# A recurrent cell on one core: VectorE's copy of the state into the operand sets becomes two

## The reference, cut to what matters

```
m = concat([x_t, h]) @ weight + bias         # 256 -> 256
c = tanh(m[128:]); g = sigmoid(m[:128] + 1)
h = g * h + (1 - g) * c                      # the output at t
```

## Time and profile before

| | us |
|---|---|
| median of 3 runs (lowest, highest) | 466.81 (466.53, 467.8) |
| the profiled execution | 467.08 |
| its span, first to last instruction | 465.3 |
| busy: PE, PEld | 347.9, 215.8 |
| busy: DVE | 345.3 (74%) |
| busy: ACT | 274.0 (59%) |
| busy: POOL | 79.4 (17%) |

### The profile page before, as it was taken

One profiled execution on the slowest core, in us unless ns is written; L12 is line 12 of the kernel. 1 busy time (PEld: TensorE's weight loads), 2 busy tenths in 40 slices (PEclk: granted clock), 3 DMA queues, 4 the chain that ended last, 5 costly groups with the idle time before them and its releaser, 6 DMA issues.

```text
span 465.3 us, 11585 instructions
## 1 busy us (share of the span) xinstructions
PE 347.9 (75%) x3776; PEld 215.8 (46%) x3776; DVE 345.3 (74%) x1940; ACT 274.0 (59%) x1020; POOL 79.4 (17%) x152
## 2 busy tenths in 40 slices
PE   1877799787846786846788988988688879777832
PEld 1644465455534453624544645535444446446510
DVE  6577666787899887899888788752851378799883
ACT  2344544436547536546656566736588888953952
POOL 6000000012000012000011100014020034266580
PEclk9999999999999999999999999995769999997966
DMA  7200920001000000000000000000000000000002
GB/s 178 61 2 25 212 40 2 1 8 41 2 0 3 0 2 1 2 1 2 0 2 2 2 1 2 2 1 3 3 2 3 1 2 4 2 0 1 23 1 68
DMA packets 9118, 8.28 MB, mean 18 GB/s; under 512 B 1282, under 2 KB 7700, under 8 KB 9060
## 3 DMA queue, kind: packets, MB, share of 16 engines
q1 hardware_dynamic: 8964, 7.29, 7.0%
q0 software_dynamic: 96, 0.26, 0.2%
HBM read 6.47 MB, written 1.08 MB: 16 GB/s over the span
## 4 chain that ended last, share of the span: by engine, by line
DVE 48%; PE 26%; ACT 14%; issue 7%; POOL 2%; DMA 1%; SPq 0%; DVEq 0%; ACTq 0%; POOLq 0%
DVE guessed L1599 8%; DVE state L1599 8%; DVE sets L1620 5%; PE zb L836 5%; DVE rest L1618 4%; ACT sets L1302 4%; PE tb L964 3%; ACT prd L1456 2%; PE firsts L1135 2%; PE tb L774 2%; PE zb L1115 2%; PE firsts L1020 1%; ACT state L1468 1%; DVE qs L1778 1%; PE tb L935 1%
## 5 line engine op out<-in xcount | busy, mean ns | idle before, releaser
L1302 ACT ACTIVATE sets<-zb 128x32 f32<-128x32 f32 x479 | 106.1, 228 | 117.9 <-PE zb L836 111.0
L836 PE MATMUL zb<-guessed,whh 128*128 128x8 f16 x960 | 64.3, 173 | 25.1 <-DVE guessed L1599 0.8
L1599 DVE TENSOR_TENSOR_SCAN state<-sets 128x32 f32<-128x32 f32 x256 | 56.9, 222 | 34.9 <-ACT sets L1302 34.5
L836 PE MATMUL zb<-rest,whh 128*128 128x8 f16 x480 | 51.6, 178 | 36.2 <-DVE rest L1618 35.1
L836 PEld LDWEIGHTS zb<-rest,whh 128*128 128x128 f16 x480 | 35.0, 112 | 87.7 <-DVE rest L1618 83.0
L1599 DVE TENSOR_TENSOR_SCAN guessed<-sets 128x32 f16<-128x32 f32 x255 | 57.6, 226 | 12.1 <-ACT sets L1302 2.9
L836 PEld LDWEIGHTS zb<-guessed,whh 128*128 128x128 f16 x960 | 44.2, 107 | 43.6 <-DVE guessed L1599 38.5
L1618 DVE TENSOR_TENSOR rest<-state,guessed 128x8 f16<-128x8 f32 x255 | 42.6, 167 | 8.7
L1456 ACT ACTIVATE prd<-zb 128x640 f32<-128x640 f32 x64 | 41.9, 711 | 5.1 <-PE zb L1115 4.4
L1620 DVE COPY sets<-state 128x32 f32<-128x32 f32 x255 | 44.8, 176 | 0.0
L630 POOL TENSOR_TENSOR stat<-mv 128x4 f32<-128x4 f32 x4 | 0.8, 209 | 220.8 <-DVE mv L1719 220.8
(11 more groups left out here) (370 smaller groups left out, 701.0 us busy)
## 6 DMA issues: line engine op xcount, KB each, us to landing
mod<-ada_rows SPq DMA_DIRECT2D x4, 768.0 KB, 11.0
resid<-in_x_dram SPq DMA_DIRECT2D x6, 128.0 KB, 3.6
ffz<-shift_rows SPq DMA_DIRECT2D x4, 131.0 KB, 3.4
out_dram<-state SPq DMA_DIRECT2D x8, 64.0 KB, 2.1
out_dram<-early SPq DMA_DIRECT2D x8, 64.0 KB, 2.1
yy<-in_L_cond_w_ada_dram SPq DMA_DIRECT2D x1, 384.0 KB
early<-in_L_cond_weight_dram SPq DMA_DIRECT2D x2, 128.0 KB
resid<-in_x_dram POOLq DMA_DIRECT2D x2, 128.0 KB, 3.5
```

The source lines that it names most:

```text
L836: return pe.matmul(bank[:, 256 * k + i:256 * k + i + NB], whh[:, half, k, :], h, start=False, stop=False, skip_group_check=True)
L1302: return act.activation(view(sets[:, n, 3:4], [39, 2], [38, 2], [4, NB]), view(bank[:, i:i + 1], [256, 2], [0, 2], [1, NB]), ACT.Tanh, sca ...
L1599: return dve.tensor_tensor_scan(dst, *scan_terms(n), 0.0, ALU.mult, ALU.add)
```

## The change

Line 1620 copied the state into places 1 and 2 of both sets, 32 elements on each partition, before the guess scan. Now VectorE copies it into set 1 alone (16 elements) at that place, and into set 0 (16 elements) behind the guess scan and ahead of the workers' instructions, counted in a new semaphore `h_kept`. Each exact scan but the first waits for `h_kept` beside `tanh_in`; before, only the last one had a second wait, on `h_copied`.

```diff
@@ semaphores
-        h_ready, h_copied = sem("h_ready"), sem("h_copied")
+        h_ready, h_copied, h_kept = sem("h_ready"), sem("h_copied"), sem("h_kept")
@@ VectorE, step(t)
                 dve.wait_ge(tanh_in, t + 1)
-                if t == STEPS - 1:
-                    dve.wait_ge(h_copied, t)
+                if t:
+                    dve.wait_ge(h_kept, t)
                 scan(h_row(t), 0).then_inc(h_ready, 1)
                 if t < STEPS - 1:
                     dve.wait_ge(h_ready, t + 1)
                     dve.tensor_tensor(rest[:, :], view(h_row(t)[:, 3:4], [4, NB]),
                                       guessed_h(t), ALU.subtract).then_inc(lo_ready, 1)
-                    dve.tensor_copy(copies_of_h(0), view(h_row(t)[:, 3:4], [0, 2], [4, NB], [0, 2]))\
+                    dve.tensor_copy(copies_of_h(1), view(h_row(t)[:, 3:4], [0, 1], [4, NB], [0, 2]))\
                        .then_inc(h_copied, 1)
                 if t + 1 < STEPS - 1:
                     guess(t + 1)
+                if t < STEPS - 1:
+                    dve.tensor_copy(view(sets[:, 0, 1:2], [4, NB], [1, 2]), view(h_row(t)[:, 3:4], [4, NB], [0, 2]))\
+                       .then_inc(h_kept, 1)
```

## The result

The changed kernel takes 474.64 us (median of 4 runs, 473.45 to 475.05), the kernel before 466.88. The ratio is 1.0159, with a 95% interval of 1.0135 to 1.0183: slower by 7.8 us where 4.05 had been forecast, and 0.6 above the upper end of the range. The direction and the main cause, VectorE being held longer, were right; the size was off by a factor of 1.9, since one term of the sum was mis-sized and one was missing.

A forecast was written before the change was run, and what follows sets the result against it. VectorE, with 48% of the chain of waits, was taken to set the end. +5.1 (VectorE-last steps) +0.65 (small margins) -1.7 (gains) = +4.05 us, giving 471.1, or 470.9 against the median; range 467.4 to 474.0.

The forecast's parts named there:

- the three kinds of steps: The 255 exact-scan steps: VectorE last in 85, tanh last with a worker's instruction on VectorE in 61, no worker in 109.
- VectorE-last steps: 85 steps whose exact scan waits for VectorE to finish a worker's instruction; forecast +60 ns each, +5.1 us together.
- The second copy is added: a hold of 77 ns: Between guess scan and workers, the new copy lasts 159 ns but delays VectorE's next start by 77 ns (58 to 85).
- hidden: Rival: behind the guess scan the second copy costs less than it seems; wholly hidden, -1.85 us, 465.0 us; chance 0.08.
- not overlapped: Rival: VectorE doesn't overlap the second copy with the next instruction, net 162 ns a step, +15 us, 482; chance 0.04.
- a shortest distance of 0.05: On VectorE, no start-to-start distance found under 0.05 us, seen behind a 4-element instruction; used against the copy being hidden.
- The first copy is halved: 17 ns saved: Ahead of the guess scan, 16 elements fewer at 1.05 ns each save 17 of 176 ns; at least 8.
- Where that gains: 1.7 us: In 110 steps where TensorE or ScalarE is late behind the guess scan, an earlier guess scan gains 15 ns each.
- the steps without a worker: 109 steps with VectorE idle 0.2 us or more before the exact scan; the second copy was to lie in that idle time.
- the small margins: 25 tanh-last steps where VectorE has under 60 ns to spare before the exact scan; uncovered delay costs 0.65 us together.
- The wait moves: nothing: Each exact scan also waits for `h_kept`, counted long before the tanh; costed at nothing.
- The rival of late scans that don't add up: Rival: a late exact scan needn't delay the next step; only 55 of 85 count, +0.7 us, 467.5; chance 0.11.

The follow-up runs named there:

- the spare copy of 16 elements: Kernel before plus, behind each guess scan, a 16-element copy into a tile nobody reads, no wait: 474.93 us beside 466.78, ratio 1.0179.
- that of 4: Kernel before plus, with no wait, a copy of 4 elements into a tile nobody reads: 474.35 us beside 466.87, ratio 1.0161.
- the first half alone: Kernel before with its copy halved to 16 elements into set 1, no second copy, no new wait: 465.99 us beside 466.78, ratio 0.9976.
- both copies and no wait: Changed kernel with the second copy going into a spare tile, so no exact scan waits for it: 472.64 us beside 466.36 for the kernel before, ratio 1.0138.
- the copies side by side: Changed kernel with the second copy moved directly behind the first, ahead of the guess scan: 466.32 us beside 466.78 for the kernel before, ratio 0.9986.
- the doubled one: Changed kernel with one more 16-element copy into a spare tile behind the second: 483.4 us beside 466.87 for the kernel before, ratio 1.0352.
- the idle waits: Kernel before with two already fulfilled waits more in each step and no other work: 469.27 us beside 466.87, ratio 1.0049.

## Why the prediction was right in kind and too low in size

- *What bounds the kernel, and the three kinds of steps.* Right. The VectorE-last steps carry 5.7 of the 7.5 us; what follows the last step changed by 0.4 us.
- *The second copy is added: a hold of 77 ns.* The number held (77 between guess scan and exact scan, 75 a step for the spare copy of 16 elements, 71 for that of 4), but in part by luck. The copy takes 151 ns, not 159, and the next instruction starts 58 behind it, at the low end of the prediction; that instruction then lasts 18 longer, for which the prediction had no term. VectorE's busy time shows the same: it grew by 14.5 us, 57 ns a copy, where the prediction had looked for 36. The rivals by which it would be hidden, or not overlapped, fell. The argument against hiding rested on a shortest distance of 0.05, and that isn't the trace's shortest: at 396.61 and 396.63 us two 4-element multiplications start 0.02 apart. The rule of the Trainium skill that the prediction weighed (VectorE: DVE Perf Modes, The DRAIN you can't avoid) would have made the hold 151; the same section adds that an instruction that isn't held starts earlier, and the 58 ns agree with that.
- *The first copy is halved: 17 ns saved.* This is the step that failed: the copy saves 7 ns. The 17 had been taken from two copies that read TensorE's results in PSUM (`firsts`), and the low end of 8, from two instructions that read and write SBUF tiles, was nearly right. The row nearest in kind was the one with the same memories, not the one with the same operation. The Trainium skill, VectorE: DVE Perf Modes, section The perf-mode tier table, says as much: an fp32 copy inside SBUF runs at 2 elements a cycle, one with a PSUM operand at 1. The runs agree, with 7 ns for 16 elements.
- *Where that gains: 1.7 us.* Failed with the same term. With 7 ns an estimate is 0.7 of gain (1.7 times 7/17), and the first half alone gained 0.6 in the steps that aren't VectorE-last. In the changed kernel the steps without a worker have a median of -2 ns, and the few of them with a stall turn their sum to +0.45 us; with both copies and no wait the same steps sum to -0.2. Putting 75 - 7 = 68 in place of 60, the sum by the prediction's own way is 85 times 68 = 5.8, plus some 1.0 for the small margins, less 0.7: +6.1. The kernel with both copies and no wait measures 6.3. So of the 3.45 us by which the steps exceeded the forecast, the mis-sized 17 ns makes about 2.
- *The wait moves: nothing.* Half right. It doesn't delay the release: an exact scan set by the tanh still starts 0.03 behind it, in some 130 steps. But where an instruction has two waits, one of them is an entry of its own in VectorE's queue, 254 in all here, and with the 255 copies the queue is 509 entries longer. The prediction counted nothing for the longer queue. The difference between 6.3 and 7.6 is 1.3 us, and the stalls of the two traces differ by about as much, 1.8 less 0.6; the two times alone would not separate it.
- *The rival of late scans that don't add up.* It was in part there: in steps 116, 124, 180, 188 and 217, the first being 0, the step is 8 to 14 ns shorter than before although the scan is 48 to 68 ns later behind its tanh. As an estimate, five steps that would each have been some 70 ns longer make 0.35 us of the sum.

What stays open: what VectorE waits for at a crossing, and why the stall is 0.05 us at one place and 0.37 at another. It isn't the number of entries alone: the kernel with the copies side by side has as many as the changed one and 1.1 us of stalls, the doubled one has 255 more and 1.0.

## What to carry to other kernels

Price an instruction on an in-order engine by how long it holds the engine, not by its duration, and look first for a place where the engine already waits for its own last result: the same copy cost 8 us behind the guess scan and nothing ahead of it. Splitting a small instruction in two saves almost nothing on the first half: here 16 of 32 elements fewer saved 7 of 176 ns. For the slope of a small operation take the row with the same memories and element type.

## What the runs showed of the hardware that was not expected

VectorE's queue is loaded in pieces, and the loads can be seen. The page has a line on instruction queue 14 among its DMA queues (packets, MB, share of the DMA engines). The kernel before:

```profile
q14 instruction: 27, 0.22, 0.2%
```

The changed kernel:

```profile
q14 instruction: 31, 0.25, 0.2%
```

With the idle waits there are 31 too. Four more for 509 more entries is one for 127, and the stalls are 128 entries apart. The packet starts behind the stalled instruction, so the crossing comes first and the load follows it. The Trainium skill, Runtime: NRT & Kernel Launch, section Instruction fetch mechanics, has engines refilled in blocks of 256 instructions and the crossing mostly hidden. In these runs VectorE's distance is half of that, and in a loop whose every step waits on VectorE the crossings took 0.5 to 2.6 us a run.
